# Last batch's pooling by blocks of 128 tokens, and one activation table for exp and tanh

## The reference, cut to what matters

```python
B, S, D, HID, A, E = 16, 512, 512, 2048, 128, 16
# layer 0: h = gelu(x @ fc1.T + b); 384 shared outputs, 128 of the batch's own expert
x = x + concat([h @ fc2_w.T + fc2_b, h @ experts_w[idx].T + experts_b[idx]])
# layer 1: attention pooling, over the tokens that batch b's type lets through
scores = tanh(x @ W1 + b1) @ v                       # [B, S]
mask = l <= j  (type 0),  l >= j  (type 1),  l != j  (type 2)
p = softmax(where(mask, scores[:, None, :], -1e30))  # [B, j, l]
x = x + einsum('bjl,bld->bjd', p, x) / count(mask)
```

## Time and profile before

| | us |
|---|---|
| median of 3 runs | 1361.4 |
| lowest and highest run | 1361.34, 1362.88 |
| the profiled execution, its own time | 1360.97 |
| span of its records (first to last instruction) | 1359.2 |
| TensorE busy (share of the span) | 1348.0 (99%) |
| VectorE busy | 1231.0 (91%) |
| ScalarE busy | 867.1 (64%) |
| mean granted TensorE clock | 1.000 |

### The profile page before, as it was taken

The page is one execution under the profiler, slowest core; times in us unless marked ns, Lnnn a source line. Parts: engine busy times, 40 slices in busy tenths (PEclk is TensorE's granted clock), DMA queues, the critical chain, the costliest instruction groups (busy, mean ns, idle before and its releaser), DMA issues.

```text
span 1359.2 us, 22001 instructions
## 1 busy us (share of the span) xinstructions
PE 1348.0 (99%) x8734; PEld 873.0 (64%) x8734; DVE 1231.0 (91%) x2057; ACT 867.1 (64%) x1493; POOL 0.2 (0%) x4
## 2 busy tenths in 40 slices
PE   9999999999999999999999999999999999999998
PEld 4448476584856748566584765848567584765856
DVE  7996889899898998989899898998989999898998
ACT  4867848377583756838477483766938468483753
POOL 0000000000000000000000000000000000000000
PEclk9999999999999999999999999999999999999999
DMA  8411011110201102010020201102010020200001
GB/s 293 150 37 33 0 63 32 42 52 1 78 17 55 40 1 78 17 62 32 20 75 1 72 24 47 48 0 78 17 62 33 8 79 9 67 27 14 25 10 55
DMA packets 29192, 62.98 MB, mean 46 GB/s; under 512 B 5922, under 2 KB 6690, under 8 KB 26658
## 3 DMA queue, kind: packets, MB, share of 16 engines
q1 hardware_dynamic: 28658, 61.05, 13.7%
q10 hardware_dynamic: 432, 0.53, 0.1%
HBM read 44.79 MB, written 16.78 MB: 45 GB/s over the span
## 4 chain that ended last, share of the span: by engine, by line
PE 90%; DVE 7%; ACT 2%; issue 0%; DMA 0%; ACTq 0%; DVEq 0%
PE ps L398 14%; PE ps L400 14%; PE ps L399 14%; PE ps L317 13%; PE ps L319 13%; PE ps L318 13%; PE ps L288 1%; PE ps L435 1%; PE ps L430 1%; PE ps L599 1%; PE ps L426 1%; PE ps L425 1%; PE ps L424 1%; DVE hl L1066 1%; DVE mx L1005 1%; DVE w2l L1066 1%
## 5 line engine op out<-in xcount | busy, mean ns | idle before, releaser
L398 PE MATMUL ps<-hh,w2l 128*128 128x512 f16 x768 | 291.1, 379 | 0.7 <-ACT ps L626 0.7
L399 PE MATMUL ps<-hh,w2h 128*128 128x512 f16 x768 | 291.1, 379 | 0.0
L400 PE MATMUL ps<-hl,w2h 128*128 128x512 f16 x768 | 291.1, 379 | 0.0
L319 PE MATMUL ps<-xh,w1l 128*128 128x256 f16 x960 | 261.7, 273 | 0.0
L318 PE MATMUL ps<-xl,w1h 128*128 128x256 f16 x960 | 261.7, 273 | 0.0
L317 PE MATMUL ps<-xh,w1h 128*128 128x256 f16 x960 | 261.7, 273 | 0.0
L651 ACT ACTIVATE g<-ps,b1s,ds 128x512 f32<-128x512 f32 x240 | 173.5, 773 | 99.5 <-PE ps L319 98.6
L317 PE MATMUL ps<-xh,ch 128*128 128x256 f16 x720 | 196.4, 273 | 0.6 <-ACT ps L626 0.3
L319 PE MATMUL ps<-xh,cl 128*128 128x256 f16 x720 | 196.3, 273 | 0.0
L318 PE MATMUL ps<-xl,ch 128*128 128x256 f16 x720 | 196.3, 273 | 0.0
L1066 DVE SCALAR_TENSOR_TENSOR hl<-g,ix,hh 128x512 f16<-128x512 f32 x244 | 177.2, 738 | 1.6
(11 more groups left out here) (208 smaller groups left out, 2337.9 us busy)
## 6 DMA issues: line engine op xcount, KB each, us to landing
xr<-in_xT SPq DMA_DIRECT2D x62, 256.0 KB, 3.1
er<-in_ew SPq DMA_DIRECT2D x15, 1024.0 KB, 5.5
out<-xr SPq DMA_DIRECT2D x60, 256.0 KB, 2.4
raw<-in_w SPq DMA_DIRECT2D x28, 256.0 KB, 6.0
er<-in_w SPq DMA_DIRECT2D x3, 1024.0 KB, 10.1
xr<-in_ew SPq DMA_DIRECT2D x1, 1024.0 KB, 6.0
out<-er SPq DMA_DIRECT2D x3, 256.0 KB, 2.5
xr<-in_xT ACTq DMA_DIRECT2D x2, 256.0 KB, 5.1
```

The lines of the kernel that those rows point to most:

```text
L319: m = mm(to, wl, mh, start=False, stop=c == 1, skip_group_check=True)
L398: mm(po(b, o), wl, hh[:, k, :], start=False, stop=False, skip_group_check=True)
L399: mm(po(b, o), wh, hh[:, k, :], start=False, stop=False, skip_group_check=True)
L400: m = mm(po(b, o), wh, hl[:, k, :], start=False, stop=k == NH - 1, skip_group_check=True)
```

## The change

Only the last batch's stage changes.

- **Blocks.** Tokens are taken in four blocks of 128. For tokens l and j of the same block, weights and products are made as before (`own_part`, three parts: `ph` x `nh`, `ph` x `nl`, `pl` x `nh`), so 15 products for the five pieces instead of 60. For l in another block, the mask passes all of the block or none of it. So the kernel makes one sum of the tokens for each block, weighted with exp(score - the block's peak): `part` (128 x 4 per block, one column filled) times `xn`, four products 4x512. A 4x512 weight `block_w` (4 blocks x 512 tokens j) multiplies those sums `block_r` (4x512): five products with four rows of contraction, in plain f32. The denominators come by `weights(t)`: two products of one column for each block, and one sum over tokens for each block, `zsum`.
- **ScalarE.** Exponentials over 512 columns (eight) become 128 columns (eight), with four of 4x128 for `block_w`, two of 128x4, and two copies out of PSUM. `see` is done once, for 128 columns.
- **VectorE.** `negative`, `weight_low` are done once each instead of four times; the sums of blocks go. Seven small instructions come in between steps of batch 14's pooling, and peaks of the blocks (`tensor_reduce` over 256 columns, twice) with four small ones among the scans. The ends are divided piece by piece. Steps of batch 14's pooling move from before the scans to behind them, the last three between the pieces' ends.
- **Tables.** L787's load of gelu's table after batch 14's exponentials and the load at L990 go: tanh, exp and the plain functions run from one table.
- **Dummies.** 17 unread products become 3.

The diff, cut:

```diff
-    ph, pl = over("ph", [P, KD, S], 16384), over("pl", [P, KD, S], 24576)
+    ph, pl = over("ph", [P, S], 16384), over("pl", [P, S], 18432)
...
+    unseen, block_w, block_r, own = pen[:, 0, 0:P], pen[0:4, 2, :], pen[0:4, 3, :], row[0]
...
-        for _ in range(17):
+        for _ in range(3):
             mm(bank[7], eh[:, 0, :], hh[:, 0, :], start=True, stop=True)
...
+        e.wait_ge(part_done, 2)
+        e.wait_ge(xn_done, KD)
+        for t in range(4):
+            m = mm(bank[7][0:4, :], part[:, 4 * t:4 * t + 4], xn[:, t, :], start=t == 0, stop=t == 3)
+        m.then_inc(sums_done)
...
+        e.wait_ge(nh_done, KD)
+        own_part(ph, nh, True, False)
+        e.wait_ge(nl_done, KD)
+        own_part(ph, nl, False, False)
+        mm(zsum, ecol, ones[:, :], start=True, stop=True).then_inc(zsum_done)
+
+        def weights(t):
+            e.wait_ge(bw_done, t + 1)
+            e.wait_ge(bz_done, 1)
+            if t == 3:
+                e.wait_ge(rz_step, 1)
+            mm(zcol[t], block_w[:, of_block(t)], block_z, start=True, stop=False, skip_group_check=True)
+            e.wait_ge(own_p_done, t + 1)
+            mm(zcol[t], own[:, of_block(t)], ones[:, :], start=False, stop=True, skip_group_check=True).then_inc(z_done)
+
+        for i, (t, d, to) in enumerate(PIECES):
+            if 0 < i < 4:
+                weights(t)
+            e.wait_ge(bw_done, t + 1)
+            e.wait_ge(br_done, 1)
+            mm(to[:, d], block_w[:, of_block(t)], block_r[:, d], start=False, stop=False, skip_group_check=True)
+            if i == 0:
+                weights(t)
+            e.wait_ge(low_done, 1)
+            mm(to[:, d], pl[:, of_block(t)], nh[:, t, d], start=False, stop=True, skip_group_check=True).then_inc(piece_done)
...
-            eng.preload_act_table(ACT.Gelu)
+            if b < LAST - 1:
+                eng.preload_act_table(ACT.Gelu)
...
-        eng.preload_act_table(ACT.Exp)
...
+        block_weight(0)
+        block_weight(1)
         for t in range(4):
-            e.wait_ge(neg_done, t + 1)
+            e.wait_ge(neg_done, 1)
             e.wait_ge(scol_done, 1)
-            act(ph[:, t, :], row[t], ACT.Exp, bias=scol[:, t:t + 1], scale=-1.0).then_inc(ph_done)
-            act(row[t], row[t], ACT.Exp, bias=scol[:, t:t + 1], scale=-1.0).then_inc(wh_done)
+            act(ph[:, of_block(t)], own[:, of_block(t)], ACT.Exp, bias=scol[:, t:t + 1], scale=-1.0).then_inc(ph_done)
+        block_weight(2)
+        block_weight(3)
+        e.wait_ge(sums_done, 1)
+        act(block_r, bank[7][0:4, :], ACT.Copy).then_inc(br_done)
+        e.wait_ge(zsum_done, 1)
+        act(block_z, zsum, ACT.Copy).then_inc(bz_done)
+        for t in range(4):
+            act(own[:, of_block(t)], own[:, of_block(t)], ACT.Exp, bias=scol[:, t:t + 1], scale=-1.0).then_inc(own_p_done)
...
+        e.wait_ge(own_p_done, 4)
+        tt(pl[:, :], own, ph[:, :].bitcast(f32), ALU.subtract).then_inc(low_done)
+        e.wait_ge(count_done, 1)
+        for n, (t, d, to) in enumerate(PIECES):
+            if n < 4:
+                e.wait_ge(z_done, t + 1)
+                tt(rz[:, t:t + 1], zcol[t], rz[:, t:t + 1], ALU.mult).then_inc(rz_step)
+                e.wait_ge(rz_step, 2 * t + 1)
+                eng.reciprocal(rz[:, t:t + 1], rz[:, t:t + 1]).then_inc(rz_step)
             e.wait_ge(piece_done, n + 1)
-            e.wait_ge(rz_step, 3)
-            stt(xn[:, q, d], to[:, d], rz[:, q:q + 1], xn[:, q, d], ALU.mult, ALU.add).then_inc(out_ready)
+            e.wait_ge(rz_step, 2 * t + 2)
+            stt(xn[:, t, d], to[:, d], rz[:, t:t + 1], xn[:, t, d], ALU.mult, ALU.add).then_inc(out_ready)
+            if n < 3:
+                pool(1)
```

More of the change, by code:

```diff
@@ L150, in build, with small, of_block @@
     eye = er[:, 0, 2 * S:2 * S + P]
+    unseen, block_w, block_r, own = pen[:, 0, 0:P], pen[0:4, 2, :], pen[0:4, 3, :], row[0]
+    def small(lo, n, parts=P):
+        return pen[0:parts, 0, P + lo:P + lo + n]
+    part, ecol, peak, rel = small(0, 16), small(16, 4), small(20, 4), small(24, 4)
+    peak_eye, reach, reach_b, block_bias, peak_col = (small(lo, 4, 4) for lo in (28, 32, 36, 40, 44))
+    open_f, open_b, block_z = (small(lo, 1, 4) for lo in (48, 49, 50))
+    zsum = po(LAST, 1)[0:4, 8:9]
+    zcol = [n[:, 16 + t:17 + t] for t, n in enumerate((po(LAST, 1), pf[1], bank[7], po(LAST, 1)))]
+    def of_block(t):
+        return slice(t * P, (t + 1) * P)
     xn = er[:, 1, :].rearrange("p (t d) -> p t d", t=4)
@@ L456, in opening, with natural_up @@
             score(b)
-        def natural_up(c, n):
+        def natural_up(c, n, halves=(0, 1)):
             e.wait_ge(eye_in, 16)
             e.wait_ge(gelu_done, nth_tile(LAST, 13 if c < 2 else 15))
-            for v in (0, 1):
+            for v in halves:
                 if c < 3:
@@ L573, in tensor_program @@
         fc2_half(1, range(12, 16))
+        e.wait_ge(nl_done, 1)
+        natural_up(3, 0, (0,))
         attend_half(1)
-        e.wait_ge(nl_done, 1)
-        natural_up(3, 0)
+        natural_up(3, 0, (1,))
         e.wait_ge(nl_done, 2)
         score_half(1, 1)
-        for v in (0, 1):
-            for t in (2 * v, 2 * v + 1):
-                m = mm(po(LAST, 1)[:, t:t + 1], att[:, t * P:(t + 1) * P], avs[:, 0:1], start=True, stop=True)
+        for t in range(4):
+            m = mm(po(LAST, 1)[:, t:t + 1], att[:, of_block(t)], avs[:, 0:1], start=True, stop=True)
@@ L602, in tensor_program @@
[L602 to L612, removed]
-            if i == 0:
[L614 to L617, removed]
-                m.then_inc(totals_done)
+        e.wait_ge(part_done, 2)
@@ new lines, in tensor_program, with own_part @@
+        e.wait_ge(xn_done, KD)
+        for t in range(4):
+            m = mm(bank[7][0:4, :], part[:, 4 * t:4 * t + 4], xn[:, t, :], start=t == 0, stop=t == 3)
+        m.then_inc(sums_done)
+        def own_part(w, x, first, last):
+            for i, (t, d, to) in enumerate(PIECES):
+                if first:
+                    e.wait_ge(ph_done, t + 1)
+                    if i == 0:
+                        e.wait_ge(nl_done, 3)
+                    if i == 4:
+                        e.wait_ge(nl_done, KD)
+                mm(to[:, d], w[:, of_block(t)], x[:, t, d], start=first, stop=last, skip_group_check=True)
@@ L1485, in vector_program @@
         ts(shift[:, :], lcol[:, :], -1.0, cD[:, i], ALU.mult, ALU.add).then_inc(shift_done)
+        for c in range(KD):
+            e.wait_ge(x_out[(LAST - 2) % XB * KD + c], x_stored(LAST - 2))
+        eng.memset(part, 0.0).then_inc(tail_small)
+        ts(open_f, cF[0:4, i], BIG, None, ALU.add).then_inc(tail_small)
+        ts(open_b, cB[0:4, i], BIG, None, ALU.add).then_inc(tail_small)
+        e.wait_ge(tail_small, 3)
+        ts(reach, io[0:4, 0:4], lcol[0:4, 0:1], open_f, ALU.is_gt, ALU.mult).then_inc(tail_small)
+        ts(reach_b, io[0:4, 0:4], lcol[0:4, 0:1], open_b, ALU.is_lt, ALU.mult).then_inc(tail_small)
+        e.wait_ge(tail_small, 5)
+        stt(reach, reach, -BIG, reach_b, ALU.add, ALU.add).then_inc(tail_small)
+        ts(rz[:, :], lcol[:, :], cntq[:, i], cntp[:, i], ALU.mult, ALU.add).then_inc(count_done)
         pool(3 + 4 + 3)
@@ L1489, in vector_program @@
         natural_low(2, 2)
-        pool(4 + 2)
+        pool(3)
         e.wait_ge(score_done, LAST + 1)
```

108 lines of the change are left out of this document (47 added, 61 removed).

## The result

| | us |
|---|---|
| changed kernel, median of 6 runs | 1367.16 |
| its lowest and highest run | 1365.40, 1367.62 |
| before, median of 6 runs (one of them took 3685.28; the others 1361.08 to 1362.88) | 1361.45 |
| ratio to before, 95% interval | 1.0039, [1.0028, 1.0050] |
| the profiled execution, its span | 1365.40, 1363.6 |

The change makes the kernel **5.7 us slower**, and the interval of the ratio leaves out 1. The forecast was 1361.6 with a range up to 1363.6, so every run lies outside it. The first line to read is the page's on TensorE: it has 31 instructions fewer and is busy for 4.4 us longer than before.

A forecast was written before the change was run, and what follows sets the result against it. TensorE was taken as the bound, with the end held by the last update and the store queue. 1353.3 + 0.76 + 3.95 + 1.4 = 1359.4 span, 0.2 longer; median 1361.6 us, range 1359.4 to 1363.6.

The forecast's parts named there:

- the clock: TensorE's last products: forecast to stay at 1.00; rival has it fall from 1343.7, 4.1 us more, 1365.5, chance 0.09.
- the piece: TensorE's full pieces at the end: denominators 0.4, block product 0.86, low part's product 0.23, together 1.5 us each.
- Seven small instructions: VectorE, behind L1485 ahead of the first scan: 1.03 us added, bounds 0.9 and 2.0, nothing hides them.
- The rival of dear small instructions: VectorE: eleven small instructions at 0.28 instead of 0.15 us plus hand-offs, 1.6 us later, 1363.2; chance 0.14.
- Penalty's end: VectorE after the scans: second maximum, small instructions and ScalarE's half add 1.1 us; ends at 1343.15, taken as 1343.0.
- Sums: TensorE's four block sums, from about 1340.2 after `part`: 0.86 us each, 3.4 in all, to 1343.7.
- VectorE's series: Divide, update and pooling step per piece at the end: claimed longer than TensorE's pieces, so block product price doesn't enter.
- The wait for `pl`: TensorE, after block product 0 and its denominators at 1346.95: waits 1.2 us for VectorE's `pl`, done at 1348.15.
- Last pooling step: VectorE, batch 14's last step, behind three updates: runs from 1352.6 to 1353.25, against an end at 1352.61 before.
- SyncE's queue: Finished pieces wait behind batch 14's last store; all 1.31 MB go out after 1353.3 in 3.95 us, end 1359.4.
- the rival without a queue: Stores at the end do not queue and the last update sets the end: 1.6 us earlier, 1359.8; chance 0.15.
- Sum on the median: Whole kernel: span 0.2 us longer, put on the median of the runs as 1361.6 us.

The follow-up runs named there:

- e1: Changed kernel with zeros filling the sums and block products to 128 columns and rows: median 1361.75 us, ratio 1.0004 to the kernel before.
- e4: Kernel before with 3 unread products instead of 17: median 1363.26 us, ratio 1.0012 to the kernel before.
- e11: Kernel before with the table change alone: median 1361.7 us, ratio 1.0001 to the kernel before.
- e7: e1 with batch 14's last three pooling steps moved ahead of `pl`: median 1361.19 us, ratio 0.9999 to the kernel before.
- e12: e10 without the zeros, same order and unread products: median 1364.33 us, ratio 1.0019 to the kernel before.
- e3: Changed kernel with 4 unread products in TensorE's wait for `pl`: median 1365.04 us, ratio 1.0027 to the kernel before.
- e5: Changed kernel with only the block products padded with zeros to 128 rows: median 1363.15 us, ratio 1.0012 to the kernel before.
- e6: Changed kernel with only the four sums padded with zeros to 128 columns: median 1366.2 us, ratio 1.0029 to the kernel before.
- e10: e7 with nine unread products instead of three ahead of the sums and four in the `pl` wait: median 1359.7 us, ratio 0.9982 to before.

## Why the prediction was wrong

The step that failed is **the clock**: "The granted clock is 1.00 up to 1359.2" was read from a kernel whose end consists of full products, and carried over to one whose end does not. The mechanism stood among the rivals, with the right reason (few rows, few columns, unread products gone) but at a chance of 0.09, and the range ended at 1363.6, below it. The text's own condition for being wrong, "if the clock in the last 15 us is not 1.00", is what happened. What it lacked was a reason for so small a chance: no row spoke for the clock holding, and the one row on a pause came with full products before and behind. With the price at 4 us and no row against it, the range should have reached it. The rival's text was wrong in one place too: "It decides only if it falls before the block products". In the profiled execution it fell behind the first of them, at 1349.6, and that was enough for 3.5 us.

The size. The rival gave 1365.5 for a fall at 1343.7, and 2.1 us for one at 1345.7. The profiled execution fell only at 1349.6 and was still 3.5 us longer than e1's (1363.6 and 1360.1). The error is in the piece: 1.5 us taken, 3.0 at half the clock; at the full clock it is 1.82 with zeros and 2.10 without, and in the changed kernel 3.75 between updates (1352.33 to 1356.08). The median is 1.8 us above the profiled run, at mean clocks of 0.993 and 0.994; by these means the clock fell earlier in those runs, which have no trace.

Now the other terms, by e1 where the clock holds. One correction first. In this pair of traces the long reciprocal of batch 14's gate, ahead of anything that the change adds, starts at 1306.65 before and at 1307.30 in the changed kernel, 0.65 later; in e1 it starts at 1307.44, 0.79 later. In traces of e4 and e11, which leave that place as it was, it starts at 1306.84 and 1307.34, and in e7 and e12, which have the change, at 1306.64 and 1306.44. So it is scatter between executions, and I take it off.

- *Seven small instructions*: forecast 1.03. In the changed kernel's timeline of VectorE:

```profile
1314.43 0.22 DVE L1523 TENSOR_SCALAR shift<-lcol,cD 128x4 f32<-128x4 f32 x1
...
1315.57 1.21 DVE L1297 TENSOR_TENSOR_SCAN raw<-raw 128x512 f32<-128x512 f32 x1
```

  1.14 us where the earlier trace rows has 0.13: 1.01. The second scan is at 1338.37, less 0.65 is 1337.7; forecast 1337.8. The rival of dear small instructions falls.
- *Penalty's end*: 1343.16, less 0.65 is 1342.5; forecast 1343.0, so the peaks and the small steps among the scans cost 0.5 us less. It changes nothing, since TensorE is in its sums until 1344.1.
- *Sums*: 0.86 each taken, 3.4 in all; 3.53 from start to start (1340.56 to 1344.09). Own products follow without a gap, as forecast.
- *The piece*: 0.4 + 0.86 + 0.23 = 1.5 taken, 2.10 measured without zeros (e3): 0.62 for the pair of one-column products (1350.59 to 1351.21), 1.05 for the block product (to 1352.26), above its upper bound of 0.86, and 0.43 for the low part's (to 1352.69). With zeros it is 1.82. So TensorE spaces the updates, and not VectorE's series, forecast at 1.70: "The price of the block product does not enter" is wrong. In e1 it costs 0.1 a piece; without zeros it would be 0.4.
- *The wait for `pl`*: forecast 1.2 us, measured 0.66 and, in e1, 0.47, since TensorE comes to it later.
- *Last pooling step*: forecast 1352.6; e1 1353.38, less 0.79 is 1352.6. *SyncE's queue*: the end forecast 1359.4; e1 1360.1, less 0.79 is 1359.3. That the stores queue is shown twice, by e1 and by the 2.2 us that e7 saves at the same clock. From the last pooling step's end to the span's end e1 has 6.0 us, forecast 6.1. So the path of the forecast was right, and the rival without a queue was not. That the last step comes out to the tenth is in part luck: the first update is 0.3 earlier than forecast (1349.08 less 0.79 is 1348.3, against 1348.55), and the two longer pieces give it back.
- *Sum on the median*: 1361.6 forecast, 1361.75 measured with zeros in place. Without zeros and with the clock held, two pieces of 2.10 instead of 1.82 make it some 1362.3, an estimate.

So what TensorE saved was real (45 of 60 products gone; the last product ends at 1354.51 in e1 and at 1355.62 before, 1.9 us earlier with the 0.79 taken off), but the queue took it back, as forecast, and what the zeros give back, 5.4 us, was lost on top, some 4.8 of it by the clock, as not forecast.

The Trainium skill, "TensorE: Matmul & The Clock Gate", Part 1, ties the clock to how busy TensorE has recently been. e4 agrees (0.50 in a pause of 4.83 us, 1.00 again under full products). e12 does not fit a reading by the busy time of the records alone: TensorE is busy for 2.00 of 2.00 us from 1342 on and its clock falls at 1350; with zeros in the rows and columns, at the same busy time, it doesn't. The records don't settle what counts: without zeros a piece of the same products also takes 2.10 instead of 1.82 us at the same clock, so the rows at rest and the slower series come together, and no run takes them apart.

Left open: whether the rows at rest or the slower series lets the clock fall; whether the sums' columns matter at all; why the pause of 1.4 us ahead of the sums lets the clock fall in the traces of e3, e5, e6 and e7 and not in those of the changed kernel and of e1 (filled, as in e10, it leaves no such spread); where it falls in the slowest runs of e5 and e7, at 0.994 and 0.995, which have no trace; whether the rounded version would be faster than e10 if its clock held; and where the clock falls in the runs at 0.993.

## What to carry to other kernels

Fewer products and fewer rows in a product are not the same saving. A product with 4 rows of contraction was not cheaper here than one with 128, and a series of them did not hold the clock. Filling the rows up with zeros and the pauses beside them with unread full products did, and each alone did not do it reliably. Look at the granted clock of the stretch before and after. And on a queue that works in order, put the step that the oldest store waits for ahead of the pieces that stand behind it: here it was worth 2.0 to 2.2 us, once the clock was held.

## What the runs showed of the hardware

- The clock can fall with TensorE busy throughout, by the records: e3 at 1354.0, e12 at 1350. Zeros in the empty rows of the block products and the empty columns of the sums, 4 and 128 against 128 and 128, keep it at 1.00 (e10). Rows and columns of zeros are enough for it.
- In this kernel the rows of the five block products decide: 4.0 us back for full rows (e5); full columns in the four sums (e6) are not told apart from none. The two stand in different places, so this is no comparison of rows with columns as such. Under products of 128 rows with 4 columns of weights the clock comes back from 0.50 to 1.00 (e3, e5, at about 1343.7).
- A pause of 1.4 us can bring the clock down and need not: in e3 it fell at 1340.3, when TensorE had been idle since 1339.5, and in the changed kernel's trace it stayed at 1.00 through a pause as long.
- Few rows save no time: a plain f32 product of 512 columns with 4 rows takes 0.96 to 1.05 us from start to start, and 1.95 to 2.00 at half the clock; the first one with 128 rows takes 1.06. In the series of a piece, 128 rows are faster: 1.82 us a piece against 2.10, and the weights behind a 4-row product are loaded 1.05 us after its start, those behind one of 128 rows after 0.51 (e3, e1).
- The level is not the same in every execution of one kernel: e7 ran between 0.994 and 1.000 and between 1359.23 and 1364.98 us, all within one set of runs. The ten runs of e10, with zeros and without pauses, lie within 0.6 us; those of the kernel before, at mean clocks of 0.999 and 1.000, lie between 1360.9 and 1363.82.
